# GpSimd waits for buffer space once per chunk of four gathers in place of once per group of sixteen

## The reference

```python
# layer 0: per edge h[src] * norm, summed per (relation, dst), then a matrix per relation
W_rel = einsum('rb,bdf->rdf', w_comp, weight)            # 32 relations from 8 bases
agg = segment_sum(h[src] * norm, etype * N + dst)
h0 = relu(einsum('rnd,rdf->nf', agg, W_rel) + h_bias + h @ loop_weight)
x = layernorm(x + h0)
# layer 1: two batch-normed products per edge, mean per dst
e = (h[dst] - h[src]) @ theta.T + h[src] @ phi.T
e = relu(bn(e, bn0)) @ fc1.T
e = relu(bn(e, bn1))
h1 = relu(segment_sum(e, dst) / max(count, 1) + h)
out = layernorm(x + h1)
```

## Time and profile before

| | |
|---|---|
| median of three runs | 3377.92 us (3369.27 to 3393.46) |
| the profiled execution | 3398.88 us, its span 3397.0 us |
| mean granted TensorE clock | 0.684 of full speed |
| busy in the span: TensorE, its weight loads | 1913.4 us, 1481.2 us |
| VectorE, ScalarE, GpSimd | 1369.8 us, 616.0 us, 1602.3 us |
| gathers of the first stage | 782, mean 950 ns, 742.7 us |
| gathers of the second stage | 782, mean 943 ns, 737.6 us |

### The profile page before, as it was taken

How to read it: one execution, slowest core, us unless ns; L and a number is a source line. 1 busy time by engine, 2 the same in 40 slices (tenths; PEclk the granted TensorE clock), 3 DMA queues, 4 the chain that set the end, 5 groups by cost and what they waited for, 6 DMA issues and landing times. The chain is left out here.

```text
span 3397.0 us, 42692 instructions
## 1 busy us (share of the span) xinstructions
PE 1913.4 (56%) x10210; PEld 1481.2 (44%) x10211; DVE 1369.8 (40%) x3584; ACT 616.0 (18%) x1004; POOL 1602.3 (47%) x1759
## 2 busy tenths in 40 slices
PE   3455555555555555544443434444444448999997
PEld 3445455554545545422222222222222223479997
DVE  4233333333333333443332333333333336877776
ACT  2111111111111111310000000000000005744444
POOL 5655555555555553335555554555555550056001
PEclk7777777777777777755555555555555558999999
DMA  3111121212112111322222222222222226924443
GB/s 81 52 53 47 51 55 48 56 46 55 46 52 53 49 52 28 97 86 84 83 83 82 82 84 80 83 84 82 81 83 82 85 84 251 306 80 147 148 148 100
DMA packets 124078, 291.18 MB, mean 86 GB/s; under 512 B 34957, under 2 KB 77506, under 8 KB 106224
## 3 DMA queue, kind: packets, MB, share of 16 engines
q1 hardware_dynamic: 65856, 136.12, 12.5%
q0 software_dynamic: 50048, 102.50, 11.6%
q10 hardware_dynamic: 8112, 51.91, 4.0%
HBM read 227.22 MB, written 63.18 MB: 85 GB/s over the span
## 5 line engine op out<-in xcount | busy, mean ns | idle before, releaser
L697 POOL DMA_INDIRECT G<-btab,srcT x782 | 737.6, 943 | 735.3 <-POOLq L56 497.8
L682 POOL DMA_INDIRECT G<-in_x,srcT x782 | 742.7, 950 | 585.9 <-POOLq L56 356.7
L906 PE MATMUL PS<-ident,G 128*128 128x128 f32 x784 | 213.0, 427 | 770.7 <-issue 426.6
L906 PEld LDWEIGHTS PS<-ident,G 128*128 128x128 f32 x784 | 140.2, 217 | 864.3 <-issue 864.3
L1477 DVE TENSOR_SCALAR ohT<-PS,node_col 80x512 bf16<-80x512 f32 x196 | 146.2, 746 | 805.8 <-issue 448.2
L780 PE MATMUL PS<-BIG,G 128*128 128x192 f32 x1564 | 362.6, 397 | 68.4 <-PEq L56 53.3
L780 PEld LDWEIGHTS PS<-BIG,G 128*128 128x128 f32 x1564 | 331.6, 239 | 83.0 <-issue 82.8
L1046 ACT ACTIVATE BIG<-PS 128x768 f32<-128x768 f32 x196 | 158.3, 809 | 1143.4 <-ACTq L56 955.0
L1313 DVE SCALAR_TENSOR_TENSOR BIG<-PS,dst0T,BIG 128x192 f32<-128x192 f32 x784 | 324.1, 416 | 77.8 <-issue 67.9
L1101 ACT ACTIVATE BIG<-PS 128x512 f32<-128x512 f32 x196 | 117.0, 597 | 1258.7 <-ACTq L56 1206.8
L1322 DVE TENSOR_TENSOR ACC<-ACC,PS 128x24 f32 x782 | 135.2, 173 | 496.0 <-DVEq L56 352.2
(11 more groups left out here) (182 smaller groups left out, 1995.2 us busy)
## 6 DMA issues: line engine op xcount, KB each, us to landing
BIG<-spill SPq DMA_DIRECT2D x90, 1024.0 KB, 4.9
spill<-BIG ACTq DMA_DIRECT2D x49, 1024.0 KB
G<-in_x,srcT POOLq DMA_INDIRECT x782
G<-btab,srcT POOLq DMA_INDIRECT x782
typ_i<-in_edge_type SPq DMA_DIRECT2D x97, 128.0 KB
BIG<-atab SPq DMA_DIRECT2D x196, 60.0 KB
atab<-BIG SPq DMA_DIRECT2D x12, 384.0 KB
xn<-in_x SPq DMA_DIRECT2D x48, 64.0 KB
```

Source lines behind the costliest of these rows:

```text
L682: nc.gpsimd.indirect_dma_start(out=G[0:n, g % 2, t, :], out_offset=None, in_=x, in_offset=bass.IndirectOffsetOnAxis(ap=srcT[0:n, TPG * g + ...
L697: nc.gpsimd.indirect_dma_start(out=G[0:n, g % 2, t, :], out_offset=None, in_=btab[:, :], in_offset=bass.IndirectOffsetOnAxis(ap=srcT[0:n, ...
L906: pe.matmul(PS[:, 2 + k, q * TILE:(q + 1) * TILE], G[:, h, TPC * k + q, :], ident[:, :], start=(q == 0), stop=False, is_transpose=True, sk ...
```

## The change

In both stages `take(pool, g_free, CPG)` ahead of a group's sixteen gathers becomes `take(pool, g_free)` ahead of each chunk's four. The buffers, the gathers, their order and every other engine's program are the same; the counts taken over a group are the same.

```diff
             def gather_x():
                 for g in range(NG):
-                    take(pool, g_free, CPG)
                     for k in range(CPG):
+                        take(pool, g_free)
                         for q in real_tiles(g, k):
...
             for g in range(NG):
-                take(pool, g_free, CPG)
                 for k in range(CPG):
+                    take(pool, g_free)
                     for q in real_tiles(g, k):
```

## The result

| | before | after |
|---|---|---|
| median, same chip | 3375.68 us (4 runs, 3369.27 to 3393.46) | 3091.79 us (4 runs, 3089.32 to 3093.85) |
| the profiled execution, its span | 3398.88 us, 3397.0 us | 3090.62 us, 3088.8 us |
| mean granted TensorE clock | 0.684 | 0.712 |

The ratio is 0.9151 [0.9115, 0.9187]: 284 us less by the medians, where 89 were forecast. The forecast had the direction, and the time is 8 us under the low end of its range.

The account below looks back on a forecast made before the run. The limit was taken to be the other engines' work in fast windows opened by GpSimd pauses. Waits 0, earlier starts 0, steady cycle -52 and -37 us sum to -89, from 3377.92 to 3289 us; range 3100 to 3470.

Parts of the forecast that it names:

- What bounds the kernel: Both gather stages: other engines nearly stand still while gathers run without pause; their work in fast windows opened by pauses is the limit.
- Step 1: Both stages: 294 more waits on GpSimd, hidden by its idle time, cost 0; at most 190 us without that cover.
- Step 2: At the second stage's fill gathers start 12 us earlier, but nobody waits for them: taken as 0.
- Step 3: Steady groups: second stage walked as 13.7 us cycles of two chunks, -52 us; first stage mean 26.2 us a group, -37 us.
- slow stretch: From some 6.2 us into a burst until 3.35 us after its last gather, others nearly stand still, yielding exactly one chunk.
- by rates: Far end of the steady cycle: 2.5 chunks per 13.7 us, 21.8 us a group, -304 us; with the first stage -400 together.
- The estimate of 24.7 us a group: Steady cycle with the skill's about 2.0 us fixed DMA cost as tail: 12.3 us a cycle; set aside for the trace's 3.35.
- What would show it: Over 90 waits a stage, about 4 us long; bursts of 8 or 12; longest drains about 10 us; groups 27 us or less.
- the two signs of being wrong: In gather bursts: the slow stretch begins at once after a restart, not some 6 us in, or doesn't end with the burst.
- the slower case: Rival, both stages: one chunk a burst of four, 34.8 us a group, +630 us if in every cycle; chance 0.24.
- No change: Rival: one long pause becomes two short ones with two 3.35 us tails, 3378 +/- 20 us; chance 0.18.
- Gathers become the bound: Rival: late space is the cause, GpSimd runs without pause at 20.0 us a group, -700 us, 2678; chance 0.08.

Follow-up runs that it names:

- break alone: Kernel before, space still taken by sixteen, plus three awaited GpSimd writes to an unused buffer between each group's eighth and ninth gather: 3125.27 us, 0.9211 of before.
- the other place: Kernel before with one wait per sixteen gathers, moved ahead of each group's third chunk, in both stages: 3350.35 us, 0.9875 of before; 1.0041 and 1.0038 on the fast chip.
- two at a time: Kernel before with one wait per two chunks (eight gathers) in both stages: 3250.14 us, 0.9579 of before; 0.9971 on the fast chip.

## Why the prediction was right in direction and short in size

**What bounds the kernel: right.** Gathers that run on end hold the other engines, and each pause opens a fast window. The break alone shows it, by making the pause and nothing else. Two things were missing. One could not be seen from one trace: the kernel alone doesn't make the holding; on one chip it isn't there. The other could: "nearly stand still" was read off one of the most held bursts. In the stretch of the earlier trace rows TensorE is busy 6%; in the same part of all 42 bursts of that stage it is 15%, and in the first stage 29%.

**Step 1, the waits at nothing: right.** On the chip without holding the changed kernel's waits leave 0.30 us between gathers in the second stage, as inside a chunk, and it is no slower than before (0.9968).

**Step 2, the earlier starts at nothing: right.** The first 48 gathers of the second stage take 91.4 us in place of 106.6, -15.2, and three groups at the steady difference of 4.31 us make 12.9 of these.

**Step 3, the steady cycle: the failed one.** It walked a cycle of 13.7 us: a burst of 8 gathers (9.68 us), and in the slow stretch exactly one chunk, which is let go 3.35 us after the burst. The mean cycle of the second stage is 13.6 us (24.24 us for 16 gathers, 782 gathers in 87 bursts, so 9.0 a burst), but that the two agree is luck: from the start of one burst to the next it is 11.6 us for the 34 of 8, 18.1 for the 30 of 12 and 7.3 for the 11 of 4. A group is thus 23.2 us by eights and 24.2 by twelves, where the walk had 27.4 and, with its tail, 24.9. The changed kernel shows where both parts of the slow stretch fail. POOL, second stage, then ScalarE's copies:

```profile
1800.62 0.94 POOL L697 DMA_INDIRECT G<-btab,srcT  x1 [2.77 <-POOLq L56]
...
1814.35 0.95 POOL L697 DMA_INDIRECT G<-btab,srcT  x1 [0.30 <-issue]
1818.81 0.94 POOL L697 DMA_INDIRECT G<-btab,srcT  x1 [3.52 <-POOLq L56]
...
1827.54 0.94 POOL L697 DMA_INDIRECT G<-btab,srcT  x1 [0.30 <-issue]
1830.49 0.94 POOL L697 DMA_INDIRECT G<-btab,srcT  x1 [2.00 <-ACTq L1099]
```

```profile
1799.95 0.60 ACT L1101 ACTIVATE BIG<-PS 128x512 f32<-128x512 f32 x1 [7.61 <-ACTq L56]
1803.70 0.60 ACT L1101 ACTIVATE BIG<-PS 128x512 f32<-128x512 f32 x1 [3.15 <-ACTq L56]
1808.75 0.60 ACT L1101 ACTIVATE BIG<-PS 128x512 f32<-128x512 f32 x1 [4.45 <-ACTq L56]
...
1818.15 0.60 ACT L1101 ACTIVATE BIG<-PS 128x512 f32<-128x512 f32 x1 [8.80 <-ACTq L56]
1821.90 0.60 ACT L1101 ACTIVATE BIG<-PS 128x512 f32<-128x512 f32 x1 [3.16 <-ACTq L56]
1829.82 0.60 ACT L1101 ACTIVATE BIG<-PS 128x512 f32<-128x512 f32 x1 [7.32 <-ACTq L56]
```

The first burst begins at 1800.62. Its second chunk comes at 1803.70, as walked. Its third comes at 1808.75, 8.1 us into the burst and in the stretch that I took as closed, while the eighth gather (1809.35) is still ahead: so the burst goes on to 12, ends at 1815.29, and the next chunk comes 2.9 us later. The second burst is the walked one of 8. It ends at 1828.48, and its held chunk is free 1.3 us later (1829.82), not 3.35: 11.7 us from start to start in place of 13.7. Over all drains of the second stage the same: behind a burst of 8 the held drain mostly ends 0.3 us before to 1.9 us after the last gather's record (median 1.1), behind 12 it is 2.4 to 2.6, behind the bursts of 16 of the kernel before mostly 2.4 to 3.3. The tail grows with the burst: in the break alone it is mostly 1.8 us behind 8 and 3.1 behind 16. I had taken it from a burst of 16 and carried it over as a constant; with 1.1 in its place the walk gives 11.4 us for a burst of 8, where 11.6 came. This is the larger part of the error. The smaller is the one chunk: in the 30 bursts of 12 a second one came. The trace of before had that too. In 24 of the 42 bursts of 16 the third chunk was freed in mid-burst, 8.7 to 16.4 us in. One of them, in the trace of before, with the copy ahead of it:

```profile
1993.29 0.60 ACT L1101 ACTIVATE BIG<-PS 128x512 f32<-128x512 f32 x1 [3.18 <-ACTq L56]
2003.36 0.60 ACT L1101 ACTIVATE BIG<-PS 128x512 f32<-128x512 f32 x1 [9.48 <-ACTq L56]
```

Its burst starts at 1990.17 and ends at 2009.83, so it comes 13.2 us in. The copy at 2013.43, which I had taken for a chunk of the slow stretch, came 3.6 us behind that burst.

How held the others are is in the busy time of three stretches of the changed kernel: the start of the burst of 12, its slow part, and the pause behind it (columns as above).

```profile
1801.00:1807.00 6.00, 5.32 (x23) 2.58 (x21) 3.58 (x7) 0.60 (x1) 4.48 (x6) 0.50 0.23 63
1808.90:1815.20 6.30, 3.07 (x12) 1.64 (x12) 2.31 (x4) 0.45 (x1) 4.78 (x6) 0.50 0.60 220
...
1815.30:1818.70 3.40, 0.15 (x1) 0.18 (x2) 0.35 (x1) 0.55 (x1) 0.00 (x0) 0.50 0.07 20
```

TensorE works 89% of the first 6 us and still 49% of the slow part; in the long burst of before it was 0.92 of 16.70 us, 6%. It isn't that a shorter burst never gets as far as that: from 8 to 12 us after the first gather TensorE is busy 3% of the time before, over its 42 bursts, and 72% in the changed kernel's bursts of 12. What differs is where the bursts stand. The third chunk's drain begins about 4 us into a burst. Before, ScalarE's 1 MB store was issued 3.3 to 4.3 us ahead of it in every burst of 16, and it lasts 4.7 to 18.3 us. At the other place and with two at a time the bursts are as long, the store is 21 us old or more, and it lasts 2.6 to 4.6. In the changed kernel eight bursts have a store 3.6 to 4.1 us old: all are of 8 gathers, and the drain lasts 5.3 to 7.5 us; 26 of the 30 bursts of 12 have one that is over 15 us old, and it lasts 2.9 to 4.6. That the store does this isn't shown: what else comes at the start of a group comes with it, bursts of 8 with a store of 12 to 15 us are held for 5 to 7 us too, and in the first stage there is no such store. It stays open. The end that I kept only for the range, by rates (21.8 us a group), was nearer in kind, though too low: 24.24 lies between it and the walk's 27.4. The estimate of 24.7 us a group that I had worked out and set aside came nearest, in part by luck: its cycle for 8 gathers is 12.3 us, and 11.6 was measured. The first stage went the same way: 24.62 us where 26.2 were forecast and 24.9 if every burst were a three. In us: -37 and -52 were forecast, -108 (2.41 x 45) and -194 (4.31 x 45) came.

**What would show it.** The drains fell to 10.6 us where "about 10" was written. The bursts are of 8 or 12 in 64 of 87 cases in the second stage and in 37 of 78 in the first, where 13 are still of 16. The waits that show as more than 0.30 us come to 62 and 73, well under the 90 a stage; most are 2.5 to 4.2 us long, some of the second stage 1.3 to 2.0. The groups of 27 us are refuted. Of the two signs of being wrong, the slow stretch begins where it should, but in the bursts of 12 it lets a chunk go before the burst ends.

**The rivals.** Bursts of four followed by a pause exist, 11 of 87, and don't go on (once two follow each other): the slower case fails at its condition, as the fast window opens again after 2 us of pause. "No change" fails by the same tails: two are not twice 3.35 us, but some 1 to 2.5 each. "Gathers become the bound" is false here, with 24 us a group, and true of the chip without holding, at 20.0, where the kernel before takes 2603 us. The Trainium skill (Perfetto Trace Analysis, Optimization Strategy) says that a gap that repeats on the engine that should be saturated can mean too little buffer space for the next tile. Here that reading would lead astray on the held chips: the break alone asks for its space as before and is 7.9% faster, and two at a time in the second stage asks for less and keeps its bursts.

## What to carry to other kernels

When a stall depends on how long something else has been running, don't carry its tail over to a shorter run as a constant, and don't read its depth off one cycle: look at all cycles of the trace, and at what else falls on their start. Walk the cycle with both ends, and let the number between them be the forecast, unless a row of the shorter run exists. When an engine waits often and its neighbours are slow only while it works, try to break its work up without giving it anything: if that alone brings the gain, the late resource was an effect and not the cause. And compare on one chip, since here the chip made a difference of 27 to 30%, over three times that of the change.

## What the runs showed of the hardware that I had not expected

- **The same kernel before takes 2603 us on one chip and 3317 to 3396 us on three others.** Where the change was compared, 17% of SP's register instructions in the kernel before and 12% after take over 0.65 us, mostly some 0.70, and 8.3 and 5.5% of VectorE's; all of these lie in the bursts or within 3 us behind one. The drain of TensorE takes up to 18.3 us. In the changed kernel on the fast chip none of SP's or VectorE's takes over 0.21 us, and no drain at L938 exceeds 2.6 us. The second stage's gathers (records of 943 ns, one each 1.248 us) are the same on both. That what is held is how the sequencers get on, and not the engines' arithmetic, is my reading of this; the register instructions of TensorE and ScalarE show nothing of it in the kernel before (none over 0.17 us), and in the changed kernel one of ScalarE's takes 0.79 us. What sets the condition, the chip or something beside it, stays open. Whether traffic or a hold-up brings it about on a chip without it wasn't tried there.
- **A gather's record hardly depends on its rows**: 943 ns for 128, 837 ns for 16, so by an estimate from these two 0.95 ns a row and some 820 ns for none (837 - 16 x 0.95).
- **Three added writes to an idle buffer per group, some 4 us on the engine that is waited for, made the kernel 7.9% faster.** In the break alone GpSimd is busy for 1886.0 us in a span of 3123.2 us; in the kernel before, on the chip of the comparison, it was 1602.3 in 3397.0.
